# Indirect gathers of embedding rows: three under way instead of two, counted on four semaphores

## The reference

```
e = stack([tbl_f[ids[:, f]] for f in range(32)], axis=1)     # 512 x 32 x 64
p, q = e[:, rows], e[:, cols]                                # the 496 pairs i < j
pij = einsum('bpe,dpe,bpd->bp', p, kernel, q)                # kernel: 64 x 496 x 64
z = pij @ W.T + b                                            # 256
h = concatenate([z, dense_ctx], axis=1)                      # 272
h = relu(h @ W_top1 + b_top1)                                # 512
h = relu(h @ W_top2 + b_top2)                                # 256
y = h @ W_top3                                               # 512 x 1
```

## Time and profile before

| | us |
|---|---|
| median of 3 runs | 285.62 |
| the runs | 281.58, 285.62, 291.13 |
| the profiled execution, its own time | 278.98 |
| its span, first to last instruction | 276.7 |

### The profile page before, as it was taken

How to read it: one execution, slowest core, us unless ns; L and a number is a source line. 1 busy time by engine, 2 the same in 40 slices (tenths; PEclk the granted TensorE clock), 3 DMA queues, 4 the chain that set the end, 5 groups by cost and what they waited for, 6 DMA issues and landing times.

```text
span 276.7 us, 3122 instructions
## 1 busy us (share of the span) xinstructions
PE 241.5 (87%) x1256; PEld 87.5 (32%) x1256; DVE 170.2 (62%) x183; ACT 24.9 (9%) x44; POOL 99.9 (36%) x109
## 2 busy tenths in 40 slices
PE   0498899809595999798999999996999999999996
PEld 0143223203142233233332333431333323333464
DVE  0397648513553868586767878766668876882121
ACT  0100111101011010201010020010010010000121
POOL 3112662375566555655663655661000000000000
PEclk9999999977979999999999999998899999999999
DMA  7997119407141325353217111110000000000000
GB/s 135 288 218 193 19 28 297 96 19 170 20 101 28 92 63 128 76 117 76 42 24 166 20 25 21 24 24 12 0 0 0 2 0 0 2 0 0 0 2 0
DMA packets 10475, 17.51 MB, mean 63 GB/s; under 512 B 3980, under 2 KB 4624, under 8 KB 10462
## 3 DMA queue, kind: packets, MB, share of 16 engines
q1 hardware_dynamic: 6056, 12.17, 17.7%
q0 software_dynamic: 3328, 3.41, 6.8%
q10 hardware_dynamic: 1078, 1.74, 2.6%
HBM read 17.31 MB, written 0.00 MB: 63 GB/s over the span
## 4 chain that ended last, share of the span: by engine, by line
PE 52%; DMA 38%; issue 5%; POOL 3%; DVE 1%; ACT 0%
DMA gathered<-in_tbl,ids_sb 38%; PE t_ps L268 25%; PE sum_ps L287 15%; POOL gathered L225 3%; PE t_ps L325 3%; PE tp_ps L294 1%; PE tp_ps L251 1%; PE t_ps L334 1%; PE t_ps L294 1%; PE t_ps L269 1%; DVE prod L417 1%; DMA ids_sb<-in_ids 1%; PE t_ps L272 1%; PE t_ps L276 1%; PE tp_ps L334 1%
## 5 line engine op out<-in xcount | busy, mean ns | idle before, releaser
L417 DVE TENSOR_TENSOR prod<-t_ps,x_sb 128x1024 f32<-128x1024 f32 x120 | 139.6, 1218 | 60.2 <-PE t_ps L269 51.6
L225 POOL DMA_INDIRECT gathered<-in_tbl,ids_sb x104 | 99.5, 957 | 87.9 <-DMA gathered<-in_tbl,ids_sb 73.0
L268 PE MATMUL t_ps<-x_sb,k_sb 64*128 64x512 f32 x240 | 116.9, 618 | 3.3 <-DVE prod L417 2.5
L269 PE MATMUL t_ps<-x_sb,k_sb 64*128 64x512 f32 x240 | 117.0, 618 | 0.0
L268 PEld LDWEIGHTS t_ps<-x_sb,k_sb 64*128 64x128 f32 x240 | 42.1, 190 | 68.9 <-issue 47.4
L287 PE MATMUL sum_ps<-prod,sel_sb 128*32 128x512 f32 x496 | 61.2, 612 | 0.0
L269 PEld LDWEIGHTS t_ps<-x_sb,k_sb 64*128 64x128 f32 x240 | 42.0, 190 | 0.0
L239 PE MATMUL tp_ps<-k_sb 125*64 125x512 f32 x108 | 27.5, 619 | 12.8 <-DVE k_sb L404 10.4
L404 DVE TENSOR_SCALAR k_sb<-ids_bc,iota_sb 125x512 f32<-125x512 int32 x54 | 22.7, 489 | 15.2 <-DMA k_sb<-in_tbl 11.3
L287 PEld LDWEIGHTS sum_ps<-prod,sel_sb 128*32 128x32 f32 x496 | 13.1, 110 | 43.5 <-issue 26.1
L251 PE MATMUL tp_ps<-ident_sb,gathered 128*128 128x128 f32 x52 | 9.3, 306 | 16.6 <-DMA gathered<-in_tbl,ids_sb 16.6
(11 more groups left out here) (35 smaller groups left out, 49.4 us busy)
## 6 DMA issues: line engine op xcount, KB each, us to landing
k_sb<-in_kern SPq DMA_DIRECT2D x32, 256.0 KB, 5.3
gathered<-in_tbl,ids_sb POOLq DMA_INDIRECT x104
ids_bc<-in_ids_t SPq DMA_DIRECT2D x6, 256.0 KB
w_sb<-in_w SPq DMA_DIRECT2D x2, 512.0 KB
k_sb<-in_tbl ACTq DMA_DIRECT2D x3, 280.0 KB
k_sb<-in_tbl ACTq DMA_DIRECT2D x3, 224.0 KB
w_pairs_sb<-in_w_pairs SPq DMA_DIRECT2D x1, 512.0 KB
ctx_sb<-in_ctx_rows SPq DMA_DIRECT2D x1, 192.0 KB
```

The lines of the kernel that those rows point to most:

```text
L225: pool.indirect_dma_start(gathered[:, n % G_RING, t, f * EMB:(f + 1) * EMB], None, tables[field], bass.IndirectOffsetOnAxis(ap=ids_sb[:, t ...
L268: pe.matmul(t[:, 0, :], k_sb[low, k, :], x_sb[low, a, :], start=True, stop=True)
L269: pe.matmul(t[:, 1, :], k_sb[high, k, :], x_sb[high, a, :], start=True, stop=True).then_inc(t_ready, 1)
L417: dve.tensor_tensor(prod[:, g % PROD_RING], t_ps[:, g % T_RING], q, ALU.mult).then_inc(prod_ready, 1)
```

## The change

The constant FLIGHT becomes 3. The semaphores `rows_in`, on which landed gathers are counted, become four, used in turn, so that their number is now a constant of its own. Gather k waits until gather k - 3 has landed, on the semaphore of that gather. PE waits on four semaphores instead of two before it turns a chunk, and each of them has counted two gathers a chunk instead of four. The number of gathers, their size, order and place are as before, as is everything on the other engines.

```
@@ -75,7 +75,8 @@
 PROD_RING = RUN + 2
 G_RING = 8
 LEAD = 3
-FLIGHT = 2
+ROWS_RING = 4
+FLIGHT = 3
 HALF = BATCH // 2
@@ -155,7 +156,7 @@
-        rows_in = [sem(f"rows_in{r}") for r in range(FLIGHT)]
+        rows_in = [sem(f"rows_in{r}") for r in range(ROWS_RING)]
@@ -221,11 +222,11 @@
                         k = (2 * n + f) * BT + t
                         if k >= FLIGHT:
-                            pool.wait_ge(rows_in[k % FLIGHT], 16 * (k // FLIGHT))
+                            pool.wait_ge(rows_in[(k - FLIGHT) % ROWS_RING], 16 * ((k - FLIGHT) // ROWS_RING + 1))
                         pool.indirect_dma_start(
                             gathered[:, n % G_RING, t, f * EMB:(f + 1) * EMB], None, tables[field],
                             bass.IndirectOffsetOnAxis(ap=ids_sb[:, t, field:field + 1], axis=0),
-                        ).then_inc(rows_in[k % FLIGHT], 16)
+                        ).then_inc(rows_in[k % ROWS_RING], 16)
@@ -246,7 +247,7 @@
                 for rows in rows_in:
-                    pe.wait_ge(rows, 16 * (n + 1) * 2 * BT // FLIGHT)
+                    pe.wait_ge(rows, 16 * (n + 1) * 2 * BT // ROWS_RING)
```

## The result

The changed kernel takes 346.91 us (median of 4, 339.49 to 349.86) against 283.6 us before; the ratio is 1.217, with a 95% interval of 1.196 to 1.238. The forecast was 269, with a range of 260 to 279. The profiled execution took 339.49 us, against 278.98. Times here and in the table are medians of all runs, while ratios and their intervals compare only runs in the faster of the two states that the chip shows, so that the two can differ a little.

The account below looks back on a forecast made before the run. Gathers were taken to set the pace up to 127.78 us, PE after that. Removing 16.0 us of PE's stops and slow clock from the 285.62 us median gave 269.6, set at 269, range 260 to 279.

Parts of the forecast that it names:

- The early supply: First gathers on POOL: third starts near 5.8 us, tenth near 28.2, 20th near 41; nine issued before 28.17, not six.
- PE's stops for gathers: PE's waits at the turns of chunks 5, 6, 7, 9 and 10: 16.6 us, to fall to about 4.
- The landings within 1.4 us of each other: Gathers 1 and 2, DMA engines full: long flight is a delay that a third gather shares, not a rate.
- the second full stretch: DMA engines full at 45 to 48 us: releases 2.84 us apart, read as a rate and used so.
- the first rival: Full DMA stretches are a rate everywhere, so a third gather only queues longer; median 279.8 us, chance 0.14.
- The supply for chunks 6 and 7: Last gathers for these turns land at 64.4 and 74.4 us, leaving PE stops of 1.0 and 2.9 us.
- the quiet stretch: POOL's gathers where DMA is not full: pace goes from 1.39 to 1.25 us, a small 0.14 us a gather.
- DVE has room: DVE is busy 44.51 of 60.22 us from 127.78 on, so PE's removed stops are not given back to it.
- The third: Rival: a third gather stretches all flights by more than half where DMA engines are full; 292.6 us, chance 0.05.
- The fourth: Rival: PE's stops go but waits for DVE or matrix slices replace them; within 2 us of 285.62, chance 0.03.
- The extra waits on PE: Two more semaphore waits at each of PE's 13 turns: between zero and 7.8 us, taken as zero.
- the sum: Gains at PE's turns: turn 7 comes 13.2 us earlier and stops of 1.76 and 1.04 go, 16.0 us altogether.

Follow-up runs that it names:

- e8: Changed kernel with three gathers under way only for the first 24 gathers, two from then on; 265.89 us against 274.32 before, ratio 0.968.
- e1: Changed kernel with two gathers under way again, still on four semaphores; 279.44 us against 278.98 before, ratio 1.006.
- e16: Changed kernel with four gathers under way and a 128x512 POOL memset behind gather 21 and later ones; 259.64 us against 279.7 before, ratio 0.940.
- e10: Changed kernel with a 128x64 POOL memset, having its own wait and increment, behind each gather; 337.74 us against 280.64 before, ratio 1.207.
- e9: Changed kernel with gathers of half a row, 128 bytes instead of 256; 344.9 us against 280.64 before.
- e18: Changed kernel with gathers of 64 rows instead of 128 and a 128x128 POOL memset behind each; 334.63 us against 279.7 before, ratio 1.210.
- e17: Changed kernel with four gathers under way and a 128x384 POOL memset behind gather 21 and later ones; 259.13 us against 279.7 before, ratio 0.928.
- e4: Changed kernel with four gathers issued in a row, then a wait until all four have landed; 286.55 us against 278.98 before, ratio 1.019.

## Why the prediction was wrong

**What held.** The early supply came as worked out: the third gather at 5.82 (forecast 5.8), the tenth at 27.75 (28.2), the twentieth at 41.45 (41). Chunk 5 was turned at 55.60 without a stop, where 54.49 was due. Quiet starts were 1.25 us apart, and PE's stops for gathers went. The landings within 1.4 us of each other were read rightly, as a delay that a third gather shares: nine gathers were issued before 27.75, not six. In the second full stretch the releases came 2.80 us apart again (the starts of 46.47 and 49.27), as taken. So the first rival did not hold for the first stretch. By the Trainium skill's rule of turns between queues ("DMA: Bandwidth & Descriptors", "Queues, rings and completion order"), as the prediction applied it, a third gather was to gain nothing there, and the trace does not agree. The supply for chunks 6 and 7 came close too: gather 32 starts at 61.12 and gather 40 at 72.87, and with the 2.6 us of flight that makes an estimate of 63.7 and 75.5 for the landings (taken: 64.4 and 74.4).

**The step that failed** is the one on the quiet stretch: "with three under way POOL never waits here and the pace is 1.25. That is 0.14 us a gather, small." The pace was right and it was priced as a gain for POOL alone. What an unbroken stream of gathers does to the others was put at nothing, without a reason. Held, it makes PE's increments late, and DVE, ACT, SP and in the end POOL itself wait for PE. The first stream, of 12 gathers from 27.75 to 42.70, is long enough to show it, though not in every run: at its end ACT copies chunk 3 1.8 us late in the changed kernel, and without delay in e8. With it fell the sentence that DVE has room, "so that the stops that go are not given back to it": 16.6 us of stops went, and 68.4 us of late releases came to DVE by the list (84.4 by pairing). With two under way it was the wait for a landing, POOL's idle time, which looked like the thing to win, that kept the mean up: from the ninth gather on, between the starts of every eighth gather of before lie 1.49 to 1.90 us a gather, and 1.35 only at the very end. In that step I took a good pair, 1.39 us, for the pace of before.

**The rivals.** The third was on the right side and wrong in kind: flights did not stretch, and POOL's wait for landings fell to 21.5 us instead of growing, which the prediction had named as its mark. The fourth had a wait for DVE in place of the stops, and PE does stand 42.7 us for DVE in the list of waits; but it was bounded at 2 us, for want of any mechanism that could make it large. The extra waits on PE, bounded at 0 to 7.8 us and taken at 0, came to 0.6% with all else of the change but the depth (e1), which is 0.2 to 2.9 us.

**What the sum is worth without the failed step.** In e16 nothing is late. Chunk 6 is turned at 63.54 without a stop (due 63.40), chunk 7 at 74.52 after a stop of 3.78 (forecast 74.4 and 2.9). The ratio of 0.940 on 279.7 us is 16.8 us (14.2 to 19.4), where 16.0 was the sum. That the numbers meet so closely is partly luck: e16 has four under way and gathers 1.66 us apart, where the sum had three and 1.25, and it has no stop at chunk 6 where the sum had 1.0. No run has three under way at 1.25 us throughout without late releases, so the sum as it stands was not tested. By an estimate from e16's ratio (0.940 x 283.6 is 267) the late releases cost the changed kernel 346.91 less 267, about 80 us.

**What stays open.** Why PE's increments are late while POOL issues a gather every 1.25 us is not settled. POOL's own are late too, by 2.6 us at one place in e10; DVE's are not, where the trace lets one see it (PE goes on 0.05 us after the products that end at 86.70, 91.62, 100.08, 110.58 and 155.38). The releases come in steps that grow (DVE's idle of 3.71, 7.23, 9.28 and 43.58 us), and the last comes 10 us after POOL's last gather of the stream, as of something piled up; that is a reading and was not tested. Whether the instruction, its semaphore increments or its descriptor work in POOL counts, e9 and e18 do not separate. The limit lies between 1.34 and 1.44 us where POOL also waits at times, and between 1.44 and 1.55 us without a break: the one late release of e17 (a wait of 4.5 us, of which 2.3 with the matmuls done) falls near 44 us, behind its unpaced first part, and its later stream at 1.55 us is clean. Between two gathers of a stream only a memset was tried as a pace; e4, e8 and the kernel before keep their mean up by waits for landings.

## What to carry to other kernels

An engine's idle time between its DMA issues can be what keeps the others running: before taking it out, ask how long the new stream goes on without a break, and hold the mean pitch of indirect gathers above the measured limit (here about 1.5 us each). Where a wait names a releaser that ended long ago, or none, look for an engine that streams meanwhile, and whose increments are late, before looking at the engine that waits. Pair the n-th consumer with the n-th producer yourself: the list's releaser is a guess by time, and it hid some 16 of 84 us here. Depth and pitch are two settings: take depth where flights are long, and pace where they are short.

## What was not expected of the hardware

- With gathers 1.25 to 1.34 us apart in the quiet stretches the kernel takes 50 to 67 us longer than before; at 1.55 to 1.66 us, four deep, it saves 15 to 20 us. With half the bytes (344.9 us) or half the rows (334.6 us) it stays slow.
- PE's increments reached ACT and DVE up to 58 us late while DVE's reached PE within 0.1 us.
- Even with two under way there are late releases, a wait of 4.03 us in e1 and one of 3.31 us in before, near the end of the gathers, where they come closest together (some 1.35 us each).
- Where a POOL memset of 128x512 runs beside them, DVE's compares take 0.80 to 0.83 us in place of 0.47 to 0.49.
